# A transformer block on one core: second modulation in ScalarE's transposed copy, router statistics by matmul, bias ranks moved to the end

## The reference

```python
mod = (_silu(c) @ wmod).reshape(8, 6, 1, 128)
sa, ca, ga, sb, cb, gb = mod[:, 0], ..., mod[:, 5]    # ga, gb: size at least 0.25
h = _layernorm(x) * (1 + ca) + sa
x = x + ga * attention(h)
h = _layernorm(x) * (1 + cb) + sb
x = x + gb * ffn(h)
# in ffn: router logits from _layernorm(h) * ln_gamma + ln_beta, then softmax over 8 experts;
# hidden = gelu(h @ W1_e + b1_e), y_e = hidden @ W2_e + b2_e, out = sum_e probs_e * y_e
# perturbed: the largest 5% by size w - 0.8 w, the smallest 5% w + 0.8 w, for W1, b1, W2, b2
```

## Time and profile before

| | |
|---|---|
| time, three runs | 238.48, 238.66, 248.0 us; median 238.66 us |
| the profiled execution | 239.84 us in all, span 238.1 us |
| granted TensorE clock | 0.978 of full speed in the mean |
| busy: PE, DVE, ACT, POOL | 216.5, 185.0, 162.6, 143.6 us |
| chain of waits | PE 63%, DVE 18%, ACT 7%, issue 7%, POOL 4% |
| DMA | 20.90 MB, HBM 86 GB/s over the span |

### The profile page before, as it was taken

How to read it: one execution, slowest core, us unless ns; L and a number is a source line. 1 busy time by engine, 2 the same in 40 slices (tenths; PEclk the granted TensorE clock), 3 DMA queues, 4 the chain that set the end, 5 groups by cost and what they waited for, 6 DMA issues and landing times.

```text
span 238.1 us, 5477 instructions
## 1 busy us (share of the span) xinstructions
PE 216.5 (91%) x1901; PEld 152.5 (64%) x1918; DVE 185.0 (78%) x562; ACT 162.6 (68%) x344; POOL 143.6 (60%) x223
## 2 busy tenths in 40 slices
PE   8977989899899899889879879979879999999993
PEld 3554757676676676666667556735535878766793
DVE  4767899889799899998998876974967585675464
ACT  2577658989989989979669769937628741453320
POOL 8650232758979979988666236437779608283600
PEclk9997999999999999999999999999985999999999
DMA  6668665965948137237036000000000001010011
GB/s 179 118 185 224 153 168 140 243 183 143 249 120 211 41 95 213 53 96 194 6 89 181 26 0 6 0 0 6 3 0 3 0 3 44 0 45 3 0 44 44
DMA packets 19461, 20.90 MB, mean 88 GB/s; under 512 B 1547, under 2 KB 17562, under 8 KB 18370
## 3 DMA queue, kind: packets, MB, share of 16 engines
q1 hardware_dynamic: 18746, 20.22, 32.5%
q10 hardware_dynamic: 688, 0.33, 0.5%
HBM read 15.16 MB, written 5.26 MB: 86 GB/s over the span
## 4 chain that ended last, share of the span: by engine, by line
PE 63%; DVE 18%; ACT 7%; issue 7%; POOL 4%; ACTq 0%; DVEq 0%; POOLq 0%
PE bank L918 12%; PE bank L898 10%; PE bank L819 6%; DVE nmax L1208 4%; PE bank L715 4%; PE bank L776 4%; ACT msk L599 3%; PE bank L798 3%; PE bank L881 3%; PE bank L772 3%; PE bank L952 3%; PE bank L824 2%; DVE msk L1183 2%; PE bank L932 2%; PE bank L930 2%
## 5 line engine op out<-in xcount | busy, mean ns | idle before, releaser
L494 POOL TENSOR_SCALAR_AFFINE_SELECT PT<-PT 128x256 f32<-128x256 f32 (+1 forms) x96 | 46.8, 502 | 35.0 <-ACT PT L584 32.8
L599 ACT ACTIVATE msk<-wa,cand 128x1024 bf16<-128x1024 f32 (+1 forms) x62 | 57.7, 941 | 5.3 <-DVE cand L1194 5.3
L584 ACT ACTIVATE PT<-bank 128x512 f32<-128x512 f32 x96 | 55.5, 607 | 5.0 <-PE bank L793 3.4
L1208 DVE TENSOR_REDUCE nmax<-bank 128x2 f32<-128x512 f32 x64 | 43.5, 685 | 2.5 <-PE bank L776 1.8
L460 POOL TENSOR_TENSOR ex<-eul,lg 128x32 f32<-128x32 f32 x4 | 21.7, 5436 | 17.2 <-DVE lg L1270 17.2
L1204 DVE TENSOR_REDUCE nmax<-bank 128x4 f32<-128x512 f32 x32 | 21.7, 677 | 4.3 <-PE bank L769 4.2
L776 PE MATMUL bank<-Ks,Qs 78*128 78x256 bf16 x128 | 24.8, 276 | 0.0
L798 PE MATMUL bank<-Qs,Ks 80*128 80x256 bf16 x128 | 24.5, 273 | 0.2 <-ACT PT L584 0.2
L1183 DVE TENSOR_SCALAR_CACHE_REDUCE msk<-wa,cand 128x512 bf16<-128x512 f32 x31 | 23.1, 746 | 1.1
L819 PE MATMUL bank<-PT,Vx 128*32 128x256 f32 x256 | 20.9, 398 | 1.6 <-POOL PT L494 1.0
L772 PE MATMUL bank<-mask 128*128 128x256 bf16 x64 | 18.0, 281 | 2.9 <-DVE nmax L1208 2.4
(11 more groups left out here) (196 smaller groups left out, 489.6 us busy)
## 6 DMA issues: line engine op xcount, KB each, us to landing
Qs<-parts SPq DMA_DIRECT2D x7, 576.0 KB
Ks<-parts SPq DMA_DIRECT2D x7, 576.0 KB
parts<-part SPq DMA_DIRECT2D x7, 384.0 KB, 2.8
rows_bc<-rows_out SPq DMA_DIRECT2D x8, 192.0 KB, 7.9
x_all<-in_x SPq DMA_DIRECT2D x8, 128.0 KB, 7.0
parts<-part SPq DMA_DIRECT2D x8, 128.0 KB, 2.9
out<-ob SPq DMA_DIRECT2D x3, 256.0 KB, 2.3
wa<-in_w SPq DMA_DIRECT2D x2, 256.0 KB, 4.6
```

The costliest lines, as they stand in the source:

```text
L494: gp.affine_select(out=v, in_=v, compare_op=ALU.is_ge, fill=0.0, base=0, pattern=[[0, v.shape[1]], [1, P]], channel_multiplier=-1).then_in ...
L584: act.activation(PT[:, e % 2, j], psE[u % 2][:, :], ACT.Exp).then_inc(q["exp_done"], 1)
L599: act.activation(scratch, wa[:, 0:width], ACT.Sign, bias=cand[:, col:col + 1].bitcast(F32), scale=-(1.0 - 2.0 ** -24), accum_out=acc[:, co ...
L1208: ve.tensor_reduce(nmax[:, b % 2, 1, h:h + 2], bank.rearrange("p (h k) -> p h k", h=2), axis=AX.X, op=ALU.max, negate=True).then_inc(q["ma ...
```

## The change

- n2 is kept for all batches and transposed as it is. The modulation 1 + cb, sb is now a scale and a bias for each channel, that is for each partition of the transposed tile: `c_act_h` does it with two activations of 128x256 (one for each batch) in place of one copy. `second_use`, the rows of it in DRAM and their eight DMAs to all partitions are gone; two small matmuls in the prologue give the columns mod2T.
- The router's statistics come from the transposed tile: a ninth column 1/128 of the router's weights gives the mean, `squares(p)` on VectorE and four one-column matmuls in `c_pe_l`, behind a wait for sq_done, give the mean square, `router_moments` makes the variance. `router_stats` is gone. `c_pe_l(0)` goes from step 36 to 33.
- The b1 masks go from GpSimd to VectorE in step 31, four in place of eight; each also sums its row, which gives the other rank. The rank matmuls (16 in place of 32) go to the end of step 32, the tiers of b1 to step 33. The masks of b2 go to step 7, its matmul behind the hidden chunk of step 31.
- `total` stands behind `pv` in every step that has both. From step 32 on the hidden chunks go ahead: before `pv` in steps 0 mod 4, and f1(1) before `ut`.
- VectorE's residual add stands ahead of rden and A. In the prologue: the first variance is added by VectorE; w_o is loaded on SyncE's queue and transposed after q and k are projected; two memsets are later; two spare matmuls fewer.

```diff
             def c_act_h(p):
...
-                act.activation(h2T[:, p % 2], (psE[1] if p >= 2 else psQ)[:, :], ACT.Copy).then_inc(q["h2T_done"], 1)
+                    act.wait_ge(q["sq_done"], p - 1)
+                for k in range(2):
+                    b = 2 * p + k
+                    act.activation(h2T[:, p % 2, S * k:S * (k + 1)], (psE[1] if p >= 2 else psQ)[:, S * k:S * (k + 1)], ACT.Identity,
+                                   scale=mod2T[:, 1, b:b + 1], bias=mod2T[:, 0, b:b + 1]).then_inc(q["h2T_done"], 1)
...
             def c_pe_l(p):
-                pe.wait_ge(q["h2T_done"], p + 1)
+                pe.wait_ge(q["h2T_done"], 2 * (p + 1))
                 claim_x((q["lg_read"], p + 1))
                 for i in range(4):
-                    last = mm(psX[:, i * NE:(i + 1) * NE], h2T[:, p % 2, i * P:(i + 1) * P], wrg[:, :], start=True, stop=True)
+                    last = mm(psX[:, i * (NE + 1):(i + 1) * (NE + 1)], h2T[:, p % 2, i * P:(i + 1) * P], wrg[:, :], start=True, stop=True)
                 last.then_inc(q["lg_psum"], 1)
+                pe.wait_ge(q["sq_done"], p + 1)
+                for i in range(4):
+                    last = mm(psX[:, MSQ_COLS + i:MSQ_COLS + i + 1], sq[:, i * P:(i + 1) * P], wrg[:, NE:NE + 1], start=True, stop=True)
+                last.then_inc(q["sq_sum"], 1)
...
-                s_unit(t, 1)
-                first = batch_at(t, AT_NMT) is not None
+                if t:
+                    s_unit(t, 1)
+                first = batch_at(t, AT_NMT) is not None and t >= B * G
                 if n is not None and first and t >= E_LAG:
                     total(n)
+                if first and t in AHEAD and t >= B * G:
+                    f1_ahead(*AHEAD[t])
                 pv(t)
...
-                if t in B1_RANKS:
-
-                    pe.wait_ge(q["b1m_done"], 2 * NC)
-                    pe.wait_ge(*free_x[0])
-                    for m in B1_RANKS[t]:
-                        k, ch = divmod(m, NC)
+                if t == BIAS_STEP + 1:
+
+                    pe.wait_ge(q["b1m_done"], 1)
+                    claim_x((q["b1p_done"], 1))
+                    for m in range(NC):
...
-            def second_use(b):
-
-                v.wait_ge(q["n2_done"], b + 1)
-                v.wait_ge(rows_in[b * ROW_DMAS // B], 32)
...
-            def router_stats(b):
...
+            def squares(p):
+
+                v.wait_ge(q["h2T_done"], 2 * (p + 1))
+                if p:
+                    v.wait_ge(q["sq_sum"], p)
+                ve.tensor_tensor(sq[:, :], h2T[:, p % 2], h2T[:, p % 2], op=ALU.mult).then_inc(q["sq_done"], 1)
...
+            def router_moments(p):
+
+                raw = psX[:, 0:4 * (NE + 1)].rearrange("p (i e) -> p i e", i=4)
+                v.wait_ge(q["sq_sum"], p + 1)
+                then_self(ve.tensor_copy(mean3[:, :], raw[:, :, NE]))
+                ve.tensor_tensor(msq3[:, :], mean3[:, :], mean3[:, :], op=ALU.mult)
+                then_self(ve.tensor_tensor(lt[:, :, :], e8(mean3[:, :]), g8(gsum[:, 0:NE]), op=ALU.mult))
+                ve.scalar_tensor_tensor(ve3[:, 4 * p:4 * p + 4], psX[:, MSQ_COLS:MSQ_COLS + 4], EPS, msq3[:, :], op0=ALU.add,
+                                        op1=ALU.subtract).then_inc(q["ln3_var"], 1)
+                ve.tensor_tensor(lg[:, :, :], raw[:, :, 0:NE], lt[:, :, :], op=ALU.subtract).then_inc(q["lg_read"], 1)
...
+            def bias_masks():
+
+                v.wait_ge(q["b1abs_done"], 1)
+                for i in range(NC):
+                    last = ve.tensor_scalar(rmask[:, i], b1a[:, :], colsa[:, i:i + 1], 0.0, op0=ALU.is_gt, op1=ALU.add,
+                                            accum_out=b1_over[:, i:i + 1])
+                last.then_inc(q["b1m_done"], 1)
...
             for n in range(2 * NPAIR):
                 combine(n)
                 p = n // 2 + 1
-                if p < NPAIR:
-                    (router_weights if n % 2 else router_logits)(p)
+                if p < NPAIR and n % 2 == 0:
+                    squares(p)
+                    router_moments(p)
+                    router_logits(p)
+                elif p < NPAIR:
+                    router_weights(p)
```

More of the change, by code:

```diff
@@ L974, in _ @@
             mm(psE[1][0:B, 0:512], c_s[:, :], wmod_sb[:, 2 * D:6 * D], start=True, stop=True).then_inc(q["pe_set"], 1)
+            pe.wait_ge(q["dve_set"], SETS["modT"])
+            for j in range(2):
+                last = mm(psE[0][:, j * B:(j + 1) * B], wmod_sb[:, (3 + j) * D:(4 + j) * D], c_s[:, :], start=True, stop=True)
+            last.then_inc(q["pe_set"], 1)
             turned(1)
@@ L1455, in _ @@
                     perturb_b2()
-            second_use(B - 1)
-            router_stats(B - 1)
+                if t == SQUARE_STEP:
+                    squares(0)
+                if t == MOMENT_STEP:
+                    router_moments(0)
             router_weights(0)
```

217 lines of the change are left out of this document (92 added, 125 removed).

## The result

The changed kernel takes 252.09 us (median of four runs, 251.1 to 253.86) against 239.13 for the kernel before in the same comparison: a ratio of 1.056, 95% interval 1.0477 to 1.0643. It is slower by 13 us. The forecast was 241.5 with a range up to 247.0. The profiled execution has a span of 248.8 us, 10.7 more than before.

A forecast was written before the change was run, and what follows sets the result against it. Steps 12 to 20 were taken as a ring of waits without a clear bound, the tail as bound by TensorE. -7.8 + 0 + 8.0 + 2.6 + 0 = +2.8 us on the 238.66 median gave 241.5 us, range 234.0 to 247.0.

The forecast's parts named there:

- start to step 32: Blocks of steps 8 to 28: less bias work, modulation and waiting leaves each near its fullest engine; 7.8 us saved.
- steps 32 to 39: Late bias work and new TensorE waits offset by removed work and half clock: 0 us, bounds -2 and +3.
- tail, at full clock: Feed-forward tail: three TensorE waits for squares, plus four more matmuls each time, cost 8.0 us; bounds 5.4 and 9.
- clock, new stretches: TensorE's clock falls to half around the new waits: 2.6 us, bounds 0 and 6.
- The total behind the weighted values: Search steps 0 mod 4: weighted values start when ScalarE's nmT copy is out, some 0.6 us sooner per block.
- The wait for b2's tiers: End of step 32: TensorE stands 3.2 us before the b1 rank matmuls, until VectorE finishes b2.
- the one for the moments: Step 34: A's transposes on TensorE wait some 2.2 us for VectorE to read the moments in bank 7.
- the half clock from 176.8 on: Steps 32 to 39: the old trace's 1.2 GHz stretch, counted among what this part no longer has.
- the three waits: Tail, c_pe_l for p = 1, 2, 3: TensorE waits for squares behind combine; costs 2.8, 3.3 and 1.9 us.
- combine, then squares: Tail on VectorE: squares(p) stands behind combine(2p-2), which can't start before f2(2p-2) ends; 1.15 and 0.69 us.
- one and a half of them: Clock lapses counted at the four new TensorE waits, each 3.5 us long and costing some 1.7 us: 2.6 us.
- Rival (a): All four new waits bring a clock lapse, 6.8 us instead of 2.6, giving 246.7 us; chance 0.14.

The follow-up runs named there:

- the first experiment: Changed kernel with squares(1), (2), (3) ahead of router_weights(0), (1), (2) on VectorE in the tail, so none stands behind a combine: 240.56 us, ratio 1.0006.
- the filled runs: Matmuls put into TensorE's waits: before the sums of squares, on the changed kernel, 246.06 us; before the b1 ranks, on the first experiment, 236.84 us.
- exponent early: Changed kernel with GpSimd's exponent of pair 0 ahead of the second normalisation of batch 6 instead of behind it: 251.94 us, ratio 1.0491.
- total in front: Changed kernel with the search's total ahead of the weighted values again in steps 0 mod 4 up to step 28: 253.8 us, ratio 1.0483.
- both moves together: Changed kernel with squares ahead of the weights in the tail and the total ahead of the weighted values up to step 28: 239.06 us, ratio 0.9932.
- the ranks alone: Changed kernel with only the b1 rank matmuls moved to the end of step 33, under the router matmuls' claim of bank 7: 247.69 us, ratio 1.0304.
- the last version: Changed kernel with squares and exponent early, total in front, ranks in step 33, moments and b1 tiers before the hidden chunk's copy in step 34: 233.39 us, ratio 0.9759.
- the total behind: Old kernel with the search's total behind the weighted values in every step, nothing else changed: 244.56 us in its one run.

## Why the prediction was wrong

Each new wait stood where it was forecast, so the mechanism of the loss was right, but four terms of the sum were off, all to the same side, and one part of the first had the wrong sign. Of the 10.7 us of the trace:

| term | forecast | trace |
|---|---|---|
| start to step 32 | -7.8 | -6.3 |
| steps 32 to 39, less the clock of the new stretch | 0 | +0.6 |
| tail, at full clock | +8.0 | +9.8 |
| clock, new stretches | +2.6 | +6.5 |
| sum | +2.8 | +10.6 |

The clock's row: half of the 3.41 us stretch is 1.7; in the tail the sums for p = 1 took 1.86 instead of 1.05, f1(3) 5.83 instead of 3.54 and f1(4) 5.24 instead of 3.54, 4.8 together.

*Steps 8 to 31: the sign of one part.* The step that failed is "The total behind the weighted values lets them start when ScalarE's nmT copy is out, some 0.6 us sooner in each block." The bias work and the rest of the change are worth 5.0 and 2.8 us by the runs, 7.8 together, the number that I had for everything. That this agrees is in part luck: the total was in that sum as one argument for it, and it costs 1.5 us. Block by block the forecast was less good than its sum. Those of steps 12 to 24 came out 0.45 to 0.5 us longer than forecast and that of step 8 0.65 longer, and step 28, called full, came out 0.9 shorter. I read an idle of ScalarE as the price of the total's place, when the earlier trace rows name the reason: the total was late because it waited for the residual add and the counts. With VectorE lighter that lateness goes by itself, and then the place in front is free, since TensorE waits for nmT there.

*Steps 32 to 39.* The wait for b2's tiers was forecast at 3.2 us and was 2.19; the one for the moments at 2.2 and was 1.36. By the sum this stretch was 0.6 longer, inside my bounds of -2 and +3, but that is luck too. I had counted the half clock from 176.8 on as something that the change takes away, but of three traces of the old kernel only this one has it. At full clock these steps take 21.9 us in the old kernel and 24.95 in the changed one, 3.1 more.

*The tail.* Forecast 2.8, 3.3 and 1.9 us for the three waits. Measured at full clock: from f2(0)'s start to the end of `c_pe_l(1)` 9.06 less 0.8 of clock, against 4.36 before, 3.9 more; from there to the end of `c_pe_l(2)` 17.88 less 2.3, 15.6 against the 15.2 that I had, 3.7 more than before; then 19.32 less 1.7, 17.6 against 17.2, 2.3 more than before. The four sums took 1.05 us each time instead of 0.8, which is 0.75 of the 1.8 that I was short. The other part is p = 1: VectorE came to combine(0) 1.7 us behind f2(0)'s end, not 1.2, and my own terms for it, 1.2 + 1.15 + 0.7 + 0.8, make 3.85 us and not the 3.6 that I wrote. (For p = 3 the slip goes the other way: 17.2 against 15.4 is 1.8, not 1.9.) The order "combine, then squares" was rightly seen as the core of the loss; the first experiment took all of it away.

*The clock.* The largest error, and the step that failed here, is "I count one and a half of them: 2.6 us, bounds 0 and 6." Three of four waits paid, and the first in the tail paid for 6.83 us instead of 3.4. Rival (a) had this mechanism with the price of 1.7 for each, and 246.7 us; it was given 0.14. The runs say that even it was too cheap: filled waits give back 6.0 us in the tail and some 3 behind the ranks, 9 us in all, where the profiled execution, the fastest of the four, shows 6.5. The profiled one had short stretches: the wait at the ranks was followed by 3.4 us at half clock in it, by 10.2 in the trace of the first experiment and by 13.7 in two others.

The trace of before could have told me of longer stretches. I took 3.5 us as the length of a lapse, but the one at 176.8, of which the earlier trace rows show the first 3.5 us, goes on in the next stretch:

```profile
180.30:183.70 3.40, 3.40 (x9) 1.76 (x8) 3.19 (x10) 2.52 (x5) 3.40 (x1) 0.50 0.02 5
```

It was 6.83 us long. Against the clock I had held the stretch at 156.4 in the earlier trace rows, after which it did not fall; one stretch without a fall was too little to halve the count on.

The reason that all terms erred to one side: I priced a gain from the fullest engine and a wait from its own length. By the filled runs the waits cost about as much again in clock as in idle: 9 us beside the 8.6 us that TensorE stood at L858 and L1051.

## What to carry to other kernels

A short operation on a helper engine that TensorE waits for in line belongs ahead of the long chain that it doesn't depend on: three VectorE instructions of 0.7 us, moved ahead of the combines, were worth 11.5 of 13 us. Price a new wait of about 2 us or more on TensorE in a full stretch at twice its length until several executions show the clock, and where the wait can't go, fill it: matmuls into an idle bank gave back 6.0 and some 3 us. And before an instruction is moved behind another to shorten a wait, ask what made it late; if that goes too, the old place may be free.

## What the runs showed of the hardware

How long TensorE stays at 1.2 GHz is not fixed by what precedes it. Six traces have the empty wait of 2.2 us at the b1 ranks, and in each the clock fell close to it, between 0.6 us ahead of its end and 1.9 us behind it: for 3.4 us (the changed kernel, and the one with filled waits in the tail), for 10.2 (squares early, exponent early) and for 13.7 (total in front, and both moves together), though TensorE was busy for all of the 10.2 us and for 13.0 and 13.2 of the 13.7. So one profiled execution prices such a wait badly, and the runs of the versions with an empty wait spread, 238.2 to 242.4 us over the ten runs of the first experiment; that is more than the 1.5 us that the place of the total is worth.

The length of the wait matters, but it is not all that decides. Five traces have the three empty waits of the tail. The second, 2.6 us, was followed by half clock in all five, for 3.4 or 6.8 us. The first was so in four (1.8 to 2.6 us; not in the run with the exponent early, where it was 1.9), and the third, 1.22 us, only in that one, for 6.8 us. The wait of 1.5 us ahead of A's transposes was followed by 6.8 us at half clock in the run with the ranks alone and by none in the version that adds squares early and the total in front to it; in the last version the clock fell for 3.4 us at 159.34 with no wait over 0.2 us since 153, behind the eight narrow matmuls of the router and the sixteen one-column ranks, which did not make it fall in the trace of the version with squares early, total in front and ranks in step 33. What made it fall there stays open. The old kernel is not free of this either: its wait of 1.31 us at the b1 ranks was followed by 13.7 us at half clock in the trace with the total behind, and by none in the trace of before.

Four matmuls with one column, each with a new f32 weight matrix, took 0.89 us together, more than four with nine columns (0.80, in the same chain): the number of columns does not set their price. The weight loads recorded with them take 0.19 us each and overlap; that they set it is likely and not shown.
